# Loads of the next rows ahead of a store's wait, and transposes and affine steps split around a sum, in the first four attention blocks of a one-core block kernel

## The chip, the cores and the metric

The kernel runs on one core of a Trainium2 chip. A core has five engines that work side by side: TensorE (PE, with its weight loads PEld), VectorE (DVE), ScalarE (ACT), GpSimd (POOL) and SyncE (SP). SP only starts transfers here; POOL also starts some. Each engine runs its instructions in program order and waits at semaphores for the others. The metric is device time in microseconds (us), lower is better: the median of several executions of the whole kernel.

## The reference, cut to what matters

Two sequences of 2048 tokens with 512 features pass through an attention-like stage and a feed-forward stage (FFN), each with a normalised and modulated input and a gated residual.

```python
mod = (silu(c) @ wmod).reshape(2, 6, 1, -1)        # sa, ca, ga, sb, cb, gb
ga, gb = sign * maximum(abs, 0.25)                 # of the gates
h = layernorm(x) * (1 + ca) + sa
# attention part:
Q = relu(rope_rotate(h @ W_Q))                     # rotates the first 64 features
H = tanh(Q + hh_b)
out = group_norm(H, 32 groups of 16) * gn_weight + gn_bias
out = swapaxes(out, -2, -1).reshape(B, T, C)       # transposed, then read as rows
x = x + ga * out
# FFN part:
h = layernorm(x) * (1 + cb) + sb
w_gate, w_up, w_down = lut[gate_idx], lut[up_idx], lut[down_idx]   # 16-entry table
x = x + gb * ((silu(h @ w_gate.T) * (h @ w_up.T)) @ w_down.T)
```

## The kernel before, in words

The 2048 tokens of a sequence are cut into four blocks of 512 tokens, and the work of a block sits in tiles of 128 partitions x 512. The kernel runs the four attention blocks of the first sequence, then the FFN in groups of two blocks, with the attention blocks of the second sequence between FFN steps. Every product with a weight is made of three float16 products (high part times high part, high times low, low times high), so every operand exists as a high and a low half.

The change is in the first part, the four attention blocks of sequence 0. The first three are called regular here (q = 0, 1, 2), the fourth is the last. Beside a block's own work these blocks build the first FFN weights: for a chunk w of 512 columns, ACT or POOL turns loaded indices into float16 (`half_idx`), DVE compares them with eight values (`masks`), PE multiplies the resulting one-hot tiles by diagonal matrices (`sum_chunk`, 16 matrix products), and ACT writes the result to the weight store (`summed_out`, four instructions). Four chunks go with each block.

A block q consists of these steps, each on one engine:

- SP loads the tokens of the block into the only buffer for it, `xa` (`load_x`); it may do so when the four transposes of the rows before are done.
- DVE computes the layer norm's numbers (`stats`), ACT applies them in place (`norm`), PE transposes the tiles (`transpose_x`, four groups k = 0 to 3 of eight instructions on two groups), ACT applies scale and shift into one of two buffers `h32` and copies the float16 high half (`affine`, in halves of two k each), POOL subtracts to get the low half (`split_lo`).
- PE multiplies by W_Q in four tiles (`project`), DVE rotates and applies the relu (`rope_relu`), ACT applies the tanh, DVE removes the group means (`center`), ACT squares, DVE sums (`sum_squares`) and scales by the group's deviation (`group_scale`, with masks of a later chunk between its small steps).
- PE transposes the result (`transpose_g`); DVE adds it to the rows in `R` (`residual`). PE's transposes k = 2 and 3 reuse the banks of 0 and 1, so they wait for the first and second of residual's four instructions.
- The rows in `R` are the input x plus a bias row that depends on the gate: SP loads x (`load_rows`), and POOL starts a transfer that accumulates the bias onto it in memory (`add_bias_rows`). `residual` waits for that transfer (semaphore `rows_added`). The bias itself is written once by ACT (`make_bias`, four instructions) and sent to `bias_dram` by SP (`store_bias`).
- SP waits for the residual and stores the rows (`x2_of_block`).

The order of all this is written out by hand in the function of each engine, so an engine's order is the order of the calls. Within a block, the steps of block q stand beside `stats`, `norm`, `transpose_x`, `affine` and `split_lo` of block q + 1, since the projection of block q + 1 needs them.

Of the kernel before, what the change touches and what calls it, by code (L numbers as in the profile page):

```python
# [95 lines left out]
def build(nc, x, wq, hh_b, gn_w, gn_b, lut, idx, c_t, wmod, cos, sin, out):  # L96
# [6 lines left out]
    with ExitStack() as ctx:  # L103
# [144 lines left out]
        def _(sp):  # L248
            def load_x(src, m):

                reach(sp, xt_ready, K * m)
                sp.dma_start(xa[:], src).then_inc(x_in, 16)
# [59 lines left out]
                sp.dma_start(bias_dram[b], bias_rows[b]).then_inc(bias_out, 16)  # L312

            for q in range(NB):
                if 0 < q < NB - 1:
                    load_x(x_toks[0, q + 1], q + 1)
                if q + 1 < NB:
                    reach(sp, x2_out, 16 * q)
                    load_rows((q + 1) % 2, rows_of_block(0, q + 1))
                last = q == NB - 1  # L320
                if last:
                    store_bias(1)
                    load_early_rows()
                if q == 0:
                    load_idx(AHEAD, 0)
                    store_bias(0)
                for w in range(AHEAD * (q + 1) + (q == 0), AHEAD * (q + 2) - last):
                    load_idx(w, w % 2)
                for s in ((), (SB,), (CB, GB), ())[q]:
                    load_mod(s)  # L330
                if not last:
                    sp.wait_ge(x2_ready, K * (q + 1))
                    sp.dma_start(x2_of_block(0, q), R[q % 2].rearrange("p (q n) -> p q n", q=A)).then_inc(x2_out, 16)
                else:
                    for k in range(K):
                        sp.wait_ge(x2_ready, K * q + k + 1)
                        src, done = ((xa[:, A - 1], x2_out), (xb[:, A - 1], x2_next))[k] if k < 2 else \
                            (R[q % 2][:, k * C:(k + 1) * C], x2_rest)
                        sp.dma_start(x2_rows[0, k][:, q], src).then_inc(done, 16)
# [72 lines left out]
        @block.gpsimd  # L412
        def _(pool):
            nc.gpsimd.memset(ident[:], 0.0).then_inc(id_zero, 1)
            pool.wait_ge(id_zero, 1)
            nc.gpsimd.affine_select(out=ident[:], in_=ident[:], compare_op=ALU.not_equal, fill=1.0, base=0,
                                    pattern=[[-1, P]], channel_multiplier=1).then_inc(id_ready, 1)
            pool.wait_ge(id_ready, 1)
            nc.gpsimd.tensor_tensor(esel[:], ident[:, 0:HALF], ident[:, HALF:P], ALU.add).then_inc(esel_ready, 1)
            pool.wait_ge(esel_ready, 1)  # L420
            pool.wait_ge(lut_split, 1)
            for h in range(2):
                for v_ in range(V):
                    ins = nc.gpsimd.tensor_scalar(diag[:, v_, h * HALF:(h + 1) * HALF], esel[:],
                                                  lutQ[:, h, v_:v_ + 1], None, ALU.mult)
            ins.then_inc(diag_ready, 1)
            pool.wait_ge(wq_max, 1)
            nc.gpsimd.partition_all_reduce(c_wqall, c_wqmax, P, RMAX).then_inc(wq_all, 1)

            def half_idx(w, par):  # L430

                reach(pool, onehot_ready, w - 1)
                pool.wait_ge(idx_in[par], (w - par) * 16 + 32)
                nc.gpsimd.tensor_scalar(idx16[par], idx_sum[par], shift[:], None, ALU.add).then_inc(idx16_late, 1)

            def split_lo(m, hi, lo, halves=(0, 1)):

                for k in (2 * h + i for h in halves for i in range(2)):
                    pool.wait_ge(hi_ready, K * m + k + 1)
                    nc.gpsimd.tensor_tensor(lo[:, k], h32[:, k % 2], hi[:, k], ALU.subtract).then_inc(lo_ready, 1)  # L440

            def table_lo(w, par):

                pool.wait_ge(w_hi, w - SUMMED + 1)
                hi, lo = (W[h][:, bass.ds(w * BLK, BLK)] for h in range(2))
                nc.gpsimd.tensor_tensor(lo, pairs[par][0], hi, ALU.subtract).then_inc(w_built, 1)

            def add_bias_rows(n, b):

                r = R_A[n] % 2  # L450
                pool.wait_ge(rows_in[r], 16 * (R_A[n] // 2 + 1))
                pool.wait_ge(bias_out, 16 * (b + 1))
                nc.gpsimd.dma_start(R[r][:], bias_dram[b], accum_op=ALU.add).then_inc(rows_added[r], 16)


            for q in range(NB - 1):
                add_bias_rows(q, 0)
                split_lo(q + 1, hq[0], hq[1])
            add_bias_rows(NB - 1, 0)
            w = AHEAD * NB  # L460
            half_idx(w + 1, 1)
            half_idx(w + 2, 0)
            split_lo(LN_B[0], h2[0][:, 0], h2[1][:, 0])
            split_lo(LN_B[1], h2[0][:, 1], h2[1][:, 1])

            for u in range(S * J):
                at = u * BLK
                pool.wait_ge(hid_hi_ready, u + 1)
                nc.gpsimd.tensor_tensor(hid[1][:, at:at + BLK], hd[:, u % S], hid[0][:, at:at + BLK],
                                        ALU.subtract).then_inc(hid_ready, 1)  # L470
                w = SUMMED + (u + 1) // 2
                if u % 2 == 0:
                    table_lo(w, w % 2)
            for g in range(G):
                if g == 1:
                    split_lo(LN_A[NB], hq[0], hq[1])
                    for n in range(NB, 2 * NB):
                        add_bias_rows(n, 1)
                        if n + 1 < 2 * NB:
                            split_lo(LN_A[n + 1], hq[0], hq[1])  # L480
                if g + 1 < G:
                    for s in range(S):
                        split_lo(LN_B[(g + 1) * S + s], h2[0][:, s], h2[1][:, s])
# [3 lines left out]
        def _(act):  # L487
# [24 lines left out]
            def tanh(n, a):  # L512
                act.wait_ge(pre_tanh, A * n + a + 1)
                nc.scalar.activation(H[:, a], H[:, a], ACT.Tanh, scale=c_isq).then_inc(tanh_ready, 1)
# [82 lines left out]
            def attn_block(q, last):  # L597
                w = AHEAD * q
                tanh(q, 0)
                if q:  # L600
                    half_idx(w + 3, 1)
                tanh(q, 1); square(q, 0); tanh(q, 2)
                if q == 0:
                    half_idx(w + 3, 1)
                square(q, 1)
                if q == 0:
                    tanh(q, 3)
                    act.wait_ge(row_ready, 1)
                    make_bias(0)
                if not last:  # L610
                    norm(q + 1)
                if q:
                    tanh(q, 3)
                summed_out(w, 0)
                square(q, 2); square(q, 3)
                if not last:
                    half_idx(w + 4, 0)
                summed_out(w + 1, 1)
                if not last:
                    affine(q + 1, CA, SA, 0, hq[0], lambda: act.wait_ge(q_ready, A * q + A))  # L620
                    half_idx(w + 5, 1)
                else:
                    half_idx(w + 4, 0)
                    copy_mod(2, (SB, CB, GB))
                summed_out(w + 2, 0)
                if not last:
                    summed_out(w + 3, 1)
                    half_idx(w + 6, 0)
# [102 lines left out]
        def _(dve):  # L731
# [294 lines left out]
            def attn_block(q, half, last):  # L1026
                w = AHEAD * q
                if q == 0:
                    rope_relu(q, q, 0)
                    gate_rows(1)  # L1030
                    rope_relu(q, q, 1)
                    gates_of_attn()
                    center(q, 0)
                    rope_relu(q, q, 2)
                    masks(w + 1, 1)
                    center(q, 1)
                    rope_relu(q, q, 3)
                else:
                    masks(w + 1, 1)
                    rope_relu(q, q, 0); rope_relu(q, q, 1); center(q, 0); rope_relu(q, q, 2); center(q, 1)  # L1040
                if not last:
                    stats(q + 1)
                if q:
                    rope_relu(q, q, 3)
# [110 lines left out]
        def _(pe):  # L1155
# [135 lines left out]
            def attn_block(q, last=False, gates=False):  # L1291
# [14 lines left out]
                if last:  # L1306
                    pe.wait_ge(q_taken, A * NB)
                    mod_product((SB, CB, GB))
                    transpose_g(q, q)
                else:  # L1310
                    transpose_x(q + 1, q)
                sum_chunk(w + 2, 0)
                if last:
                    mod_vec(2, (SB, CB))
                if not last:
# [126 lines left out]
```

## Time and profile before

| | us |
|---|---|
| median of 3 runs | 1008.93 (1008.84 to 1010.18) |
| the profiled execution, its time | 1010.04 |
| the profiled execution, its span | 1008.2 |
| PE busy | 924.3 (92%) |
| DVE busy | 597.6 (59%) |
| ACT busy | 432.1 (43%) |
| POOL busy | 137.1 (14%) |

The span runs from the first to the last instruction of the profiled execution. The regular attention blocks lie between about 40 and 169 us of it; the FFN's matrix products begin at 249.67 us. An average over the span hides that: the three blocks are another kind of work than the rest, and the change is only there. A timeline row reads: start, duration, engine, line, operation, output from input, shape, number of instructions merged, and in brackets how long the engine sat idle before and what released it.

### The profile page before, as it was taken

How to read it: one execution, taken by the hardware profiler on the slowest of the kernel's cores; microseconds unless marked ns; L12 is line 12 of the kernel's file. 1: busy time of each engine (PE TensorE's matmuls, PEld its weight loads, DVE VectorE, ACT ScalarE, POOL GpSimd, SP SyncE). 2: the span in 40 equal slices, each digit the busy share in tenths (PEclk: the TensorE clock that was granted, in tenths of full speed). 3: DMA queues.
4: the chain of work that ended last, by engine and by line, in shares of the span. 5: the costliest groups of instructions: out<-in, count | busy, mean ns of one | idle time of the engine just before them, and what ended most of it. 6: DMA issues, size and time to landing. Idle time of an engine off the chain costs nothing.

```text
span 1008.2 us, 12879 instructions
## 1 busy us (share of the span) xinstructions
PE 924.3 (92%) x4364; PEld 431.8 (43%) x4364; DVE 597.6 (59%) x1379; ACT 432.1 (43%) x652; POOL 137.1 (14%) x127
## 2 busy tenths in 40 slices
PE   4948668868999999999999999999999999999998
PEld 1324334333444444444444444444444444444443
DVE  5988989994899983338988863322223332222312
ACT  2475757468877742256255233312223331222200
POOL 3011202033333321122022001100000110000000
PEclk9969788989999999999999999999999999999999
DMA  8658365720000032240533314230000212000001
GB/s 283 189 125 230 99 193 167 236 78 32 22 21 26 15 136 84 92 136 13 167 72 98 81 47 194 74 104 0 0 0 1 73 42 95 0 0 0 11 32 42
DMA packets 33738, 83.44 MB, mean 83 GB/s; under 512 B 2848, under 2 KB 2976, under 8 KB 30624
## 3 DMA queue, kind: packets, MB, share of 16 engines
q1 hardware_dynamic: 32544, 74.54, 22.4%
q0 software_dynamic: 1152, 8.39, 4.5%
q8 instruction: 21, 0.34, 0.1%
q14 instruction: 21, 0.17, 0.1%
HBM read 64.04 MB, written 18.87 MB: 82 GB/s over the span
## 4 chain that ended last, share of the span: by engine, by line
PE 68%; DVE 16%; ACT 6%; issue 5%; DMA 5%; SPq 0%; POOL 0%; DVEq 0%; ACTq 0%
PE ps L1211 33%; PE ps L1247 22%; PE ps L1200 4%; DMA xa<-x_dram 4%; PE ps L1178 3%; DVE hid L846 3%; DVE st L765 2%; PE ps L1166 2%; PE ps L1223 2%; DVE R L832 1%; ACT xa L493 1%; ACT w_all L555 1%; ACT h L503 1%; PE ps L1258 1%; DMA w_all<-wmod_dram 1%
## 5 line engine op out<-in xcount | busy, mean ns | idle before, releaser
L1211 PE MATMUL ps<-h,w_all 128*128 128x512 f16 x1920 | 416.5, 379 | 3.3 <-ACT w_all L555 2.5
L1211 PEld LDWEIGHTS ps<-h,w_all 128*128 (+1 forms) x1920 | 187.7, 98 | 229.5 <-ACT w_all L555 3.0
L1247 PE MATMUL ps<-w_all,hid 128*128 128x512 f16 x1056 | 229.7, 379 | 0.4 <-DVE w_all L1093 0.4
L1247 PEld LDWEIGHTS ps<-w_all,hid 128*128 128x128 f16 x1056 | 103.3, 98 | 123.9 <-issue 0.9
L889 DVE SCALAR_TENSOR_TENSOR hd<-ps,col,sg 128x512 f32<-128x512 f32 x80 | 59.9, 749 | 128.7 <-ACT sg L525 128.3
L525 ACT ACTIVATE sg<-ps,col 128x512 f32<-128x512 f32 x80 | 54.8, 685 | 170.6 <-PE ps L1211 170.3
L914 DVE SCALAR_TENSOR_TENSOR hd<-ps,col,gbB 128x512 f32<-128x512 f32 x32 | 24.0, 751 | 140.5 <-PE ps L1247 140.1
L493 ACT ACTIVATE xa<-xa,ln_sb 128x512 f32<-128x512 f32 x60 | 44.0, 805 | 125.9 <-DVE ln_sb L775 125.9
L1200 PE MATMUL ps<-hid,w_all 128*128 128x512 f16 x352 | 89.1, 415 | 8.1 <-DVE hid L846 8.0
L540 ACT ACTIVATE hid<-hd 128x512 f16<-128x512 f32 (+1 forms) x88 | 55.0, 628 | 85.7 <-DVE hd L889 69.7
L1178 PE MATMUL ps<-WQ,work 128*128 128x512 f16 x384 | 85.4, 379 | 6.3 <-DVE work L794 3.2
L440 POOL TENSOR_TENSOR h<-h,h 128x512 f16<-128x512 f32 x32 | 38.3, 1217 | 305.1 <-ACT h L510 305.1
L846 DVE TENSOR_SCALAR hid<-hid 128x1024 f16<-128x1024 f16 x176 | 70.8, 461 | 15.0 <-PE ps L1200 15.0
L1166 PE MATMUL ps<-ident,xa 128*128 128x128 f32 x240 | 36.3, 301 | 42.6 <-ACT h L503 26.3
L907 DVE TENSOR_TENSOR hid<-hd,hid 128x512 f32 (+1 forms) x66 | 45.3, 691 | 47.5 <-ACT hid L540 47.5
L503 ACT ACTIVATE h<-ps,vec 128x512 f32<-128x512 f32 x64 | 47.7, 775 | 40.5 <-PE ps L1166 20.5
L440 POOL TENSOR_TENSOR work<-h,work 128x512 f16<-128x512 f32 x28 | 35.2, 1276 | 200.0 <-ACT work L510 189.1
L1200 PEld LDWEIGHTS ps<-hid,w_all 128*128 128x128 f16 x352 | 36.9, 106 | 57.4 <-issue 14.7
L1178 PEld LDWEIGHTS ps<-WQ,work 128*128 128x128 f16 x384 | 37.0, 98 | 51.9 <-DVE work L794 4.7
L555 ACT ACTIVATE w_all<-ps 64x512 f16<-64x512 f32 x88 | 52.1, 592 | 12.3 <-PE ps L1200 11.3
L1166 PEld LDWEIGHTS ps<-ident,xa 128*128 128x128 f32 x240 | 30.1, 154 | 50.9 <-ACT h L503 28.2
L765 DVE BATCH_NORM_STATS2 st<-xa 128x6 f32<-128x512 f32 x60 | 37.0, 681 | 7.7 <-DMA xa<-x_dram 7.6
(116 smaller groups left out, 766.1 us busy)
## 6 DMA issues: line engine op xcount, KB each, us to landing
R<-x_dram SPq DMA_DIRECT2D x16, 1024.0 KB, 6.9
xa<-x_dram SPq DMA_DIRECT2D x14, 1024.0 KB, 5.6
hid<-idx_dram SPq DMA_DIRECT2D x44, 256.0 KB, 5.5
R<-bias_dram POOLq DMA_DIRECT2D x8, 1024.0 KB, 9.0
out_dram<-R SPq DMA_DIRECT2D x32, 256.0 KB, 2.2
x_dram<-R SPq DMA_DIRECT2D x7, 1024.0 KB, 5.1
w_all<-wmod_dram SPq DMA_DIRECT2D x6, 1024.0 KB, 13.2
h<-idx_dram SPq DMA_DIRECT2D x11, 256.0 KB, 2.6
```

What stands on the lines that cost most here:

```text
L440: nc.gpsimd.tensor_tensor(lo[:, k], h32[:, k % 2], hi[:, k], ALU.subtract).then_inc(lo_ready, 1)
L503: nc.scalar.activation(h32[:, k % 2], bank(banks[k % len(banks)]), ACT.Identity, bias=vec[:, shift, k, b:b + 1], scale=vec[:, scale, k, b: ...
L540: nc.scalar.activation(hid[0][:, bass.ds((j * S + s) * BLK, BLK)], hd[:, s], ACT.Copy) \
L555: ins = nc.scalar.activation(W[h][rows, bass.ds(w * BLK, BLK)], bank(GU[2 * par + half])[h * HALF:(h + 1) * HALF], ACT.Copy)
L765: ins = v.bn_stats(st[:, a], x_[:, a])
L846: ins = v.tensor_scalar(onehot[par][:, v_], idx16[par], float(v_), None, ALU.is_equal)
L889: v.scalar_tensor_tensor(hd[:, s], bank(GU[2 * s + 1]), c_kappa, sg[:, s], ALU.mult, ALU.mult) \
L1166: ins = nc.tensor.transpose(bank(banks[k % len(banks)])[:, a * P:(a + 1) * P], x_[:, a, k * P:(k + 1) * P], ident[:])
L1178: ins = nc.tensor.matmul(bank(QY[a % 2]), hq[hp][:, k, a * P:(a + 1) * P], WQ[wp][:, k], start=(k == 0 and i == 0), stop=(k == K - 1 and i ...
L1200: ins = nc.tensor.matmul(bank(GU[2 * par + half]), diag[:, v_], onehot[par][:, v_, half], start=v_ == 0, stop=v_ == V - 1)
L1211: ins = nc.tensor.matmul(bank(GU[2 * s + t]), W[wp][:, bass.ds(at, P)], h2[hp][:, s, k], start=(k == 0 and i == 0), stop=(k == K - 1 and i ...
L1247: ins = nc.tensor.matmul(bank(QY[par]), hid[hp][:, bass.ds(at, P)], W[wp][:, w_at:w_at + BLK], start=(j == 0 and i == 0), stop=(j == J - 1 ...
```

## The change

Five edits, all for sequence 0:

- SP: block q + 2's tokens are loaded ahead of the wait for block q's residual, not behind its store.
- POOL: the first accumulation of the bias (block 0) stands behind block 1's `split_lo`, not ahead of it. The others keep their places.
- ACT, block 0: `make_bias` stands behind `norm`, a square and the first `summed_out`, not ahead of them; the square of tile 1 stands behind `norm`.
- DVE, block 0: `stats` of block 1 stands ahead of `center` of tile 1.
- PE and ACT, blocks 0 to 2: the second half of `transpose_x` stands behind the third chunk's sum, and the second half of `affine` behind that chunk's `summed_out`.

```diff
@@ SP @@
             for q in range(NB):
-                if 0 < q < NB - 1:
-                    load_x(x_toks[0, q + 1], q + 1)
                 if q + 1 < NB:
                     reach(sp, x2_out, 16 * q)
                     load_rows((q + 1) % 2, rows_of_block(0, q + 1))
...
                 for w in range(AHEAD * (q + 1) + (q == 0), AHEAD * (q + 2) - last):
                     load_idx(w, w % 2)
+                if q + 2 < NB:
+                    load_x(x_toks[0, q + 2], q + 2)
                 for s in ((), (SB,), (CB, GB), ())[q]:
                     load_mod(s)
@@ POOL @@
-            for q in range(NB - 1):
+            for q in range(1, NB):
+                split_lo(q, hq[0], hq[1])
+                if q == 1:
+                    add_bias_rows(0, 0)
                 add_bias_rows(q, 0)
-                split_lo(q + 1, hq[0], hq[1])
-            add_bias_rows(NB - 1, 0)
@@ ACT @@
                 if q == 0:
                     half_idx(w + 3, 1)
-                square(q, 1)
-                if q == 0:
                     tanh(q, 3)
+                    norm(q + 1)
+                    square(q, 1)
+                    summed_out(w, 0)
                     act.wait_ge(row_ready, 1)
                     make_bias(0)
-                if not last:
-                    norm(q + 1)
-                if q:
+                else:
+                    square(q, 1)
+                    if not last:
+                        norm(q + 1)
                     tanh(q, 3)
-                summed_out(w, 0)
+                    summed_out(w, 0)
...
                 if not last:
-                    affine(q + 1, CA, SA, 0, hq[0], lambda: act.wait_ge(q_ready, A * q + A))
+                    affine(q + 1, CA, SA, 0, hq[0], lambda: act.wait_ge(q_ready, A * q + A), halves=(0,))
                     half_idx(w + 5, 1)
+                    summed_out(w + 2, 0)
+                    affine(q + 1, CA, SA, 0, hq[0], lambda: None, halves=(1,))
                 else:
                     half_idx(w + 4, 0)
                     copy_mod(2, (SB, CB, GB))
-                summed_out(w + 2, 0)
+                    summed_out(w + 2, 0)
@@ DVE @@
                     masks(w + 1, 1)
+                    rope_relu(q, q, 3)
+                    stats(q + 1)
                     center(q, 1)
-                    rope_relu(q, q, 3)
...
-                if not last:
+                if q and not last:
                     stats(q + 1)
@@ PE @@
-                    transpose_x(q + 1, q)
+                    transpose_x(q + 1, q, halves=(0,))
                 sum_chunk(w + 2, 0)
+                if not last:
+                    transpose_x(q + 1, q, halves=(1,))
```

POOL, from its last step before block 0 to the accumulation for block 2. `R<-bias_dram` is the accumulating transfer of `add_bias_rows`, `work<-h,work` the subtraction of `split_lo`.

```order
 L428 ISA col<-col 128x1
-L453 DMA R<-bias_dram 128x2048
 L440 ISA
 L440 TENSOR_TENSOR work<-h,work 128x512 x4
-L453 DMA R<-bias_dram 128x2048
+L453 DMA R<-bias_dram 128x2048 x2
 L440 TENSOR_TENSOR work<-h,work 128x512 x4
 L453 DMA R<-bias_dram 128x2048
```

The first accumulation, for block 0, now stands behind the four subtractions of block 1 and directly ahead of the one for block 1.

ACT in block 0, from the last tanh to the end of the block: first before, then now. L493 and L494 are `norm`, L519 and L520 `square`, L555 and L556 `summed_out`, L577 and L578 `make_bias`, L503/L510 and L504/L511 `affine`, L547 and L548 `half_idx`.

```order
L577 ACTIVATE h_0<-gaB,gnb 128x512 x4
L493 ACTIVATE xa<-xa,ln_sb 128x512 x4
L555 ACTIVATE w_all<-ps 64x512 x4
L519 ACTIVATE sq<-work 128x512 x2
L547 ACTIVATE hid<-hid,shift 128x1024
L555 ACTIVATE w_all<-ps 64x512 x4
L503 ACTIVATE h<-ps,vec 128x512 x2
L510 ACTIVATE work<-h 128x512 x2
L503 ACTIVATE h<-ps,vec 128x512 x2
L510 ACTIVATE work<-h 128x512 x2
L547 ACTIVATE hid<-hid,shift 128x1024
L555 ACTIVATE w_all<-ps 64x512 x8
```

```order
L494 ACTIVATE xa<-xa,ln_sb 128x512 x4
L520 ACTIVATE sq<-work 128x512
L556 ACTIVATE w_all<-ps 64x512 x4
L578 ACTIVATE h_0<-gaB,gnb 128x512 x4
L520 ACTIVATE sq<-work 128x512 x2
L548 ACTIVATE hid<-hid,shift 128x1024
L556 ACTIVATE w_all<-ps 64x512 x4
L504 ACTIVATE h<-ps,vec 128x512 x2
L511 ACTIVATE work<-h 128x512 x2
L548 ACTIVATE hid<-hid,shift 128x1024
L556 ACTIVATE w_all<-ps 64x512 x4
L504 ACTIVATE h<-ps,vec 128x512 x2
```

`make_bias` stands five instructions later, and between the two halves of `affine` there now are one `half_idx` and one `summed_out`; the last two copies and the fourth `summed_out` follow.

## Rows read from the trace of the kernel before

**Rows 1.** Windows: busy time of each engine, granted clock (PEclk), DMA

```profile
81.20:124.30 43.10, 31.31 (x145) 15.57 (x144) 38.72 (x107) 28.01 (x42) 6.77 (x5) 0.84 0.59 168
250.00:1008.00 758.00, 743.25 (x3584) 348.05 (x3581) 391.90 (x810) 279.41 (x424) 90.38 (x77) 1.00 0.17 56
```

**Rows 2.** Chain of waits, its piece behind block 0's residual and store: start, us, what

```profile
81.66 10.74 DMA xa<-x_dram
```

**Rows 3.** Timeline of DVE, blocks 0 to 2

```profile
45.10 2.77 DVE L846 TENSOR_SCALAR hid<-hid 128x1024 f16<-128x1024 f16 x8
...
73.68 4.70 DVE L846 TENSOR_SCALAR hid<-hid 128x1024 f16<-128x1024 f16 x8 [2.28 <-PE ps L1200]
78.31 2.90 DVE L832 SCALAR_TENSOR_TENSOR R<-ps,gnw,R 128x512 f32<-128x512 f32 x4
...
85.70 0.24 DVE L790 TENSOR_TENSOR gs<-ps,cosT 128x64 f32<-128x64 f32 x1 [0.43 <-PE ps L1178]
...
92.43 2.47 DVE L765 BATCH_NORM_STATS2 st<-xa 128x6 f32<-128x512 f32 x4 [1.21 <-DMA xa<-x_dram]
...
117.51 3.61 DVE L846 TENSOR_SCALAR hid<-hid 128x1024 f16<-128x1024 f16 x8 [1.15 <-PE ps L1200]
121.48 2.91 DVE L832 SCALAR_TENSOR_TENSOR R<-ps,gnw,R 128x512 f32<-128x512 f32 x4 [0.36 <-PE ps L1190]
...
136.80 2.47 DVE L765 BATCH_NORM_STATS2 st<-xa 128x6 f32<-128x512 f32 x4 [2.28 <-DMA xa<-x_dram]
161.88 3.62 DVE L846 TENSOR_SCALAR hid<-hid 128x1024 f16<-128x1024 f16 x8 [1.15 <-PE ps L1200]
```

**Rows 4.** Timeline of ACT, block 0, and one row of block 1

```profile
51.24 2.55 ACT L577 ACTIVATE h<-gaB,gnb 128x512 f32<-128x512 f32 x4
55.79 2.93 ACT L493 ACTIVATE xa<-xa,ln_sb 128x512 f32<-128x512 f32 x4 [2.00 <-DVE ln_sb L775]
...
61.18 1.15 ACT L519 ACTIVATE sq<-work 128x512 f32<-128x512 f32 x2
62.35 1.15 ACT L547 ACTIVATE hid<-hid,shift 128x1024 f16<-128x1024 int32 x1
63.52 2.40 ACT L555 ACTIVATE w_all<-ps 64x512 f16<-64x512 f32 x4
65.95 1.45 ACT L503 ACTIVATE h<-ps,vec 128x512 f32<-128x512 f32 x2
67.30 1.15 ACT L510 ACTIVATE work<-h 128x512 f16<-128x512 f32 x2
...
110.58 1.15 ACT L510 ACTIVATE work<-h 128x512 f16<-128x512 f32 x2
```

**Rows 5.** Timeline of POOL, blocks 0 and 1

```profile
71.27 2.27 POOL L440 TENSOR_TENSOR work<-h,work 128x512 f16<-128x512 f32 x2 [10.87 <-issue]
75.01 2.76 POOL L440 TENSOR_TENSOR work<-h,work 128x512 f16<-128x512 f32 x2 [1.47 <-ACT work L510]
77.72 1.05 POOL L453 DMA_DIRECT2D R<-bias_dram  x1
...
115.35 3.13 POOL L440 TENSOR_TENSOR work<-h,work 128x512 f16<-128x512 f32 x2 [1.47 <-ACT work L510]
```

**Rows 6.** DMA issued at 59.19, 77.72 and 118.44: KB, us to landing

```profile
R<-bias_dram POOLq DMA_DIRECT2D x1, 1024.0 KB, 9.3
...
R<-bias_dram POOLq DMA_DIRECT2D x1, 1024.0 KB, 9.2
...
R<-bias_dram POOLq DMA_DIRECT2D x1, 1024.0 KB, 12.7
```

**Rows 7.** Windows after an idle stretch of PE: PE busy first, PEclk third from last

```profile
66.78:68.75 1.97, 1.97 (x9) 1.85 (x10) 1.94 (x8) 1.66 (x3) 0.00 (x0) 0.50 0.97 216
68.75:73.60 4.85, 4.85 (x18) 1.89 (x16) 2.59 (x3) 0.78 (x1) 2.27 (x2) 0.71 0.08 18
73.60:77.10 3.50, 3.50 (x19) 1.68 (x17) 3.42 (x7) 3.45 (x6) 2.09 (x2) 1.00 0.00 0
```

## The prediction

> **What bounds the kernel now.** I read the windows first. From 250 us on PE is busy 743.25 of 758.00 us at full clock, while in block 1's stretch it is busy 31.31 of 43.10 us and DVE 38.72 [rows 1]. So in the regular blocks DVE sets the pace, and the change can only return what DVE sits idle there, plus what a new wait costs. What the blocks win or lose is handed on whole to the FFN, which starts on what they leave.
>
> Then the waits and the timeline of DVE, for its idle time. It waits twice for the tokens of the next block, 1.21 us in block 1 and 2.28 in block 2 [rows 3], 3.5 in all. Behind each block's last group step it waits 1.15 us for a sum of PE, and in block 1 another 0.36 for the transposes ahead of `residual` [rows 3]. The chain of waits shows where the tokens' lateness comes from: block 0's residual ends at 81.21 (78.31 + 2.90) [rows 3], the store is issued, and the load behind it, at 81.66, takes 10.74 us [rows 2].
>
> Last the timelines of ACT and POOL in block 0 and the landing times, for the step that `residual` waits for and that none of the above waits shows: the accumulation of the bias. Before, the first one was issued at 59.19 and took 9.3 us [rows 6], so it was there at 68.5, ten microseconds ahead of the residual at 78.31 [rows 3].
>
> **Part 1: the load of tokens ahead of the wait.** It leaves SP when the index loads of the block are out and the transposes done, some 8 us earlier in block 0 and more in block 1. The cover that it needs is there: `stats` of block 2 could not start before 91.2 (92.43 less 1.21) [rows 3]. Both waits go: -1.21 and -2.28, together -3.5 us. The instructions are the same; what is behind it on SP, the store, waits for the residual anyway.
>
> **Part 2: the halves in blocks 1 and 2.** The third sum now fills PE's wait for the first affine half and is over before DVE's group step, so the 1.15 us go, and the 0.36 with them: at most 1.5 us a block. But ACT now does a `half_idx` (1.15) and a `summed_out` (2.40) between the halves [rows 4]. In block 1's own clock: the first copies end at 111.73 [rows 4], + 1.15 + 2.40 + 1.45 for the affine pair (adding up to 116.7), and POOL begins about 0.6 later, at 117.3, where it began at 115.35 [rows 5]. That puts all of its 3.13 us beside DVE's masks, which can start at 116.36 (117.51 less 1.15) [rows 3]. What such overlap costs is in block 0: eight masks take 2.77 alone and 4.70 where POOL's 2.76 lie inside them [rows 3, 5], so in these 2.76 us DVE got through 0.83 us of masks, 30%. Here: 0.94 us free, then 3.13 us at 30% (0.94), then the remaining 0.89 us: they end near 121.3, where the residual before started at 121.48. So the halves give 0.2 us a block, not 1.5. With no overlap cost it would be 1.5 (plus 0.8 for the overlap of before, 3.61 less 2.77); with POOL running later still, -0.5. I take 0.2 each, -0.4 for two blocks, bounds -4.6 to +1.
>
> **Part 3: block 0.** Here I follow ACT. `stats` moves ahead of one `center` (two DVE steps, about 1.3 us), so `norm` starts at about 54.5 instead of 55.79 and ends at 57.4. Then a square 0.6, `summed_out` 2.40 (60.5), `make_bias` 2.55 (63.05), two squares (64.3), `half_idx` 1.15 (65.45), `summed_out` 2.40 (67.85), first affine half 1.45 and copies 1.1 (70.4), `half_idx` 1.15 (71.55), `summed_out` 2.40 (73.95), second half's affine pair 1.45, and the copies from 75.3 [durations from rows 4]. POOL starts its last two subtractions at about 76.0 and needs 2.6 to 3.1 us: 78.9.
>
> POOL's 10.87 us of issue ahead of its first subtraction [rows 5] begin behind the transfer at 59.19; now nothing stands between and they fall in the idle time before. That was worth about 3 us to ACT's second half (copies from 67.30, subtraction at 71.27 and not 68.0), and is given back by the steps put between. The residual could start at about 78.5, as before.
>
> But it can't, since the accumulation for its rows is now issued only at 78.9. The two accumulations without other traffic took 9.3 and 9.2 us, the one beside a modulation load, a store and a token load 12.7 [rows 6]. In the new place the token load is out since about 73 and nearly landed; only the second accumulation follows 1.1 us behind, on the same queue. I take 9.3: landing at 88.2, against a residual at 78.31. DVE waits there, PE's third transpose stands behind the residual, and block 1's projection behind that: nothing hides it. +9.9 us, bounds +8 (POOL done at 77.5, landing 9.0) and +13.3 (12.7).
>
> A page speaks against this size. The Trainium skill ("DMA: Bandwidth & Descriptors", section on the anatomy of one DMA on the SWDGE path) gives a transfer issued from GpSimd about 2.0 us plus the bytes at 436 GB/s; an estimate by that page for 1 MB is 4.4 us. The trace does not agree for the accumulating transfer, which took 9.2 us and more each time. By the page the total below would be about 5 us lower.
>
> **Part 4: PE's clock behind the new wait.** PE has its first two transpose groups done by about 77 and then nothing until 88.9. After an idle stretch of only 6 us before, its granted clock was 0.50 and then 0.71 of full: 1.97 + 4.85 us went into work that at clock 1.00 takes about 1.0 (half of 1.97) + 3.50 (16 products of a sum, as in the next window) [rows 7]. So 2.3 us are lost, on the third and fourth transposes and the first tiles of block 1's projection. DVE has masks (2.77) to do meanwhile, but it waited 0.43 us for tile 1 before, with PE at full clock [rows 3], so all of it comes through: +2.3, bounds 0.9 and 3.
>
> **Sum** against the profiled execution: -3.5 - 0.4 + 9.9 + 2.3 = +8.3 us. Its time is 1010.04, so 1018.3; the median of the runs is 1.1 lower, and on its scale the time is 1008.93 + 8.3 = 1017.2. I forecast 1017.
>
> **Rivals.**
> - *The accumulation is hidden after all.* If it were on chip by the time of the residual, only parts 1 and 2 and their better case would remain: -3.5 and -0.4 to -3: 1002.5 to 1005, say 1004.5. For it: POOL's long issue time goes, and ACT's second half could run earlier than I have it. Against it: it would have to be issued by 69, and four subtractions whose inputs ACT makes after 73.95 stand ahead of it. It decides from the point at which issue plus 9.3 is earlier than 78.5. 8%.
> - *The loss is there, but smaller.* The accumulation moves 1 MB and nothing competes with it; if it takes half of the shortest row, 4.6 us, the sum is 4.6 less: +3.7, 1012.6. Against it: that row, 9.2, was issued into idle queues too [rows 6]. 8%. The Trainium skill's rule above ("DMA: Bandwidth & Descriptors") leads to this case.
> - *The gains are larger.* POOL's subtractions do not hit the masks: -1.5 -0.8 twice instead of -0.4: 1017.2 - 4.2 = 1013. For it: the masks' start at 116.36 and POOL's at 117.3 are each known to half a microsecond only. 12%.
> - *The landing is slow.* The second accumulation's packets go between the first's, and it takes the 12.7 of the loaded case: +3.4, 1020.5. 12%.
> - *The token load in front of the store brings nothing*, since a later step was going to hold DVE anyway: +3.5, also near 1020.5. In the trace nothing ends within these waits but the load, so only 3%.
>
> **Chances.** The forecast, 1015 to 1019, has 57%, the rivals 43%. The 80% range leaves out the hidden case and the tails of the others: 1011.5 to 1020.7. About 0.2%, 2 us, is what a measurement can tell. Faster than 1006.9: only the first rival, 8%. Within 2 us: the corner of the second and third together, 7%. Slower: 85%.
>
> **What would show it.** In the changed profile DVE's first instruction of `residual` in block 0 should have about 10 us of idle time before it, released by the DMA from `bias_dram`, and start near 88. POOL's accumulations should stand together near 79 and 80. PE's granted clock should fall to 0.5 near 89, with block 1's second tile late by 12 us. The waits for `xa` should be gone. In blocks 1 and 2 the eight masks ahead of the residual should have no idle time before them but last 4 to 5 us. I am wrong if the first accumulation is issued before 70 or lands within 6 us, or if residual 0 starts by 80; and if block 1 takes under 40 us from residual to residual, part 2 was undervalued.

## The result: 1.1% slower

| | before | changed |
|---|---|---|
| median of 4 runs each, us | 1009.17 | 1019.74 (1019.34 to 1022.11) |
| profiled execution, us | 1010.04 | 1019.6 |
| its span, us | 1008.2 | 1017.8 |

The ratio of changed to before is 1.0108, with a 95% interval of 1.009 to 1.0125. Measured again later it was 1.0107 (1.0092 to 1.0121). The forecast was 1017 us, or 8.3 us more than before, with 1011.5 to 1020.7 as its range; measured were 10.6 us more between the medians and 9.6 between the profiled executions.

The step on which most of it rested is in DVE's timeline of the changed kernel, which answers to [rows 3]. L837 is now `residual`, L851 `masks`, L795 the first step of `rope_relu`, L770 `stats`.

```profile
74.07 4.68 DVE L851 TENSOR_SCALAR hid<-hid 128x1024 f16<-128x1024 f16 x8
86.41 1.41 DVE L837 SCALAR_TENSOR_TENSOR R<-ps,gnw,R 128x512 f32<-128x512 f32 x2 [7.66 <-DMA R<-bias_dram]
...
95.33 0.23 DVE L795 TENSOR_TENSOR gs<-ps,cosT 128x64 f32<-128x64 f32 x1 [1.11 <-PE ps L1184]
...
100.75 2.46 DVE L770 BATCH_NORM_STATS2 st<-xa 128x6 f32<-128x512 f32 x4
...
124.61 4.69 DVE L851 TENSOR_SCALAR hid<-hid 128x1024 f16<-128x1024 f16 x8
129.22 1.39 DVE L837 SCALAR_TENSOR_TENSOR R<-ps,gnw,R 128x512 f32<-128x512 f32 x2
131.16 1.60 DVE L837 SCALAR_TENSOR_TENSOR R<-ps,gnw,R 128x512 f32<-128x512 f32 x2 [0.55 <-PE ps L1196]
...
138.90 0.23 DVE L795 TENSOR_TENSOR gs<-ps,cosT 128x64 f32<-128x64 f32 x1 [1.11 <-PE ps L1184]
```

DVE sat idle 7.66 us ahead of block 0's residual, until the bias accumulation had landed. `stats` at 100.75 has no wait in brackets: the wait for the tokens is gone. Both sets of masks ahead of a residual run without a wait, but for 4.7 us instead of 2.77. And the rope steps of the second tile (the two with L795) each have 1.11 us of waiting for PE.

POOL's timeline (answers to [rows 5]) and one piece of the chain of waits show the accumulation: two are issued from 78.09, and the first takes 8.30 us.

```profile
69.33 2.34 POOL L440 TENSOR_TENSOR work<-h,work 128x512 f16<-128x512 f32 x2 [45.98 <-ACT work L511]
75.54 2.60 POOL L440 TENSOR_TENSOR work<-h,work 128x512 f16<-128x512 f32 x2 [3.86 <-ACT work L511]
78.09 2.09 POOL L453 DMA_DIRECT2D R<-bias_dram  x2
```

```profile
78.09 8.30 DMA R<-bias_dram
```

PE's timeline around the residuals of blocks 0 and 1. L1196 is `transpose_g`, eight instructions for two of the four groups, and L1184 the projection of the next block.

```profile
87.22 1.97 PE L1196 MATMUL ps<-ident,work 128*128 128x128 f32 x8 [11.06 <-DVE R L837]
88.98 11.42 PE L1184 MATMUL ps<-WQ,work 128*128 128x512 f16 x48
...
130.01 1.97 PE L1196 MATMUL ps<-ident,work 128*128 128x128 f32 x8 [4.01 <-DVE R L837]
131.77 12.20 PE L1184 MATMUL ps<-WQ,work 128*128 128x512 f16 x48
```

In block 1 of the kernel before, where L1190 is `transpose_g` and L1178 the projection, the same instructions read:

```profile
120.76 1.04 PE L1190 MATMUL ps<-ident,work 128*128 128x128 f32 x8
122.28 1.32 PE L1190 MATMUL ps<-ident,work 128*128 128x128 f32 x8 [0.49 <-DVE R L832]
123.56 10.53 PE L1178 MATMUL ps<-WQ,work 128*128 128x512 f16 x48
```

There the second eight transposes take 1.32 us and the projection 10.53, with a granted clock of 1.00 and a gap of only 0.49 us ahead of them. In the changed kernel PE was idle 11.06 us ahead of the first and 4.01 us ahead of the second, and both were followed by slow work. The windows of the changed kernel behind the second (columns as in [rows 7]) put the granted clock at 0.50 and 0.60.

```profile
130.00:131.80 1.80, 1.79 (x9) 1.73 (x10) 1.25 (x2) 0.48 (x1) 0.00 (x0) 0.50 1.08 284
131.80:136.00 4.20, 4.20 (x13) 1.57 (x12) 3.54 (x10) 0.00 (x0) 0.00 (x0) 0.60 0.92 192
```

How far DVE is behind the kernel before, at the same instructions of both profiled executions, gives the sum by terms. The last column tells what accounts for the change from the row above it.

| instruction of DVE | before | changed | behind | what lies between |
|---|---|---|---|---|
| residual 0 | 78.31 | 86.41 | 8.10 | late accumulation, +8.1 |
| rope of tile 1, block 1 | 85.70 | 95.33 | 9.63 | slow clock, +1.5 |
| stats for block 2 | 92.43 | 100.75 | 8.32 | wait for tokens gone, -1.3 |
| residual 1 | 121.48 | 129.22 | 7.74 | halves, -0.6 |
| rope of tile 1, block 2 | 129.01 | 138.90 | 9.89 | slow clock, +2.2 |
| stats for block 3 | 136.80 | 144.32 | 7.52 | wait for tokens gone, -2.4 |
| residual 2 | 165.85 | 172.78 | 6.93 | halves, -0.6 |
| rope of tile 1, block 3 | 173.26 | 182.86 | 9.60 | slow clock, +2.7 |
| end of the span | 1008.2 | 1017.8 | 9.6 | nothing |

### The profile page after: what moved, and what is told of

It reads as the page before. It is cut to its first block, busy times and chain, and to the rows that moved or that the text cites. A ratio compares the mean times of both kernels' runs of the same rounds, so it can differ in the third digit from the quotient of the medians.

```text
span 1017.8 us, 12880 instructions
## 1 busy us (share of the span) xinstructions
PE 930.6 (91%) x4364; PEld 432.2 (42%) x4364; DVE 605.1 (59%) x1379; ACT 430.3 (42%) x652; POOL 135.3 (13%) x127
## 4 chain that ended last, share of the span: by engine, by line
PE 66%; DVE 19%; ACT 6%; issue 5%; DMA 4%; POOL 1%; SPq 1%; DVEq 0%; ACTq 0%; POOLq 0%
PE ps L1217 33%; PE ps L1253 22%; PE ps L1184 4%; DVE hid L851 4%; DVE st L770 2%; PE ps L1229 2%; DMA xa<-x_dram 1%; ACT xa L494 1%; DMA w_all<-wmod_dram 1%; PE ps L1172 1%; PE ps L1206 1%; DVE R L837 1%; ACT w_all L556 1%; DVE gs L758 1%; ACT h L504 1%
## 5 line engine op out<-in xcount | busy, mean ns | idle before, releaser
L494 ACT ACTIVATE xa<-xa,ln_sb 128x512 f32<-128x512 f32 x60 | 44.0, 803 | 123.3 <-DVE ln_sb L780 123.3
L1184 PE MATMUL ps<-WQ,work 128*128 128x512 f16 x384 | 90.0, 393 | 4.5 <-DVE work L799 3.2
L851 DVE TENSOR_SCALAR hid<-hid 128x1024 f16<-128x1024 f16 x176 | 76.6, 493 | 6.6 <-PE ps L1206 6.6
L504 ACT ACTIVATE h<-ps,vec 128x512 f32<-128x512 f32 x64 | 47.4, 774 | 33.2 <-PE ps L1172 20.5
L1184 PEld LDWEIGHTS ps<-WQ,work 128*128 128x128 f16 x384 | 38.4, 101 | 53.6 <-issue 8.2
L556 ACT ACTIVATE w_all<-ps 64x512 f16<-64x512 f32 x88 | 52.0, 590 | 9.5 <-PE ps L1206 8.5
L1172 PE MATMUL ps<-ident,xa 128*128 128x128 f32 x240 | 32.8, 281 | 16.7 <-ACT xa L494 10.0
L515 ACT ACTIVATE work<-work,col 128x512 f32<-128x512 f32 x32 | 23.0, 719 | 55.1 <-DVE work L801 55.1
L1196 PE MATMUL ps<-ident,work 128*128 128x128 f32 x128 | 19.9, 304 | 25.0 <-DVE R L837 19.1
```

Source lines behind the costliest of these rows:

```text
L494: ins = nc.scalar.activation(x_[:, a], x_[:, a], ACT.Identity, bias=ls[:, 3, a:a + 1], scale=ls[:, 2, a:a + 1])
L504: nc.scalar.activation(h32[:, k % 2], bank(banks[k % len(banks)]), ACT.Identity, bias=vec[:, shift, k, b:b + 1], scale=vec[:, scale, k, b: ...
L556: ins = nc.scalar.activation(W[h][rows, bass.ds(w * BLK, BLK)], bank(GU[2 * par + half])[h * HALF:(h + 1) * HALF], ACT.Copy)
L851: ins = v.tensor_scalar(onehot[par][:, v_], idx16[par], float(v_), None, ALU.is_equal)
L1184: ins = nc.tensor.matmul(bank(QY[a % 2]), hq[hp][:, k, a * P:(a + 1) * P], WQ[wp][:, k], start=(k == 0 and i == 0), stop=(k == K - 1 and i ...
```

## The experiments

Each is given with its ratio to the kernel before in runs on the same chip, and the 95% interval. The kernel before had medians of 1010.38, 1010.26 and 1010.23 us in the three batches, with single runs from 1008.0 to 1013.6.

### Block 0 undone

```diff
 # the kernel before, plus: load_x of q + 2 ahead of the wait for residual q,
 # transpose_x and affine in halves around the third sum
 # as before: add_bias_rows(0) ahead of split_lo(1), make_bias ahead of norm
```

> The kernel before with the early token loads and the halves on PE and ACT, but with block 0 on POOL, ACT and DVE as before (bias accumulation ahead of the subtractions, make_bias early). My theory: the loss of block 0 comes from the late accumulation, so it goes; of the rest, the two token waits give 3.5 us and the overlap gain 1.2, and PE's slow clock behind the idle gap that the halves open costs 2 us or more in each block: 1009 to 1012. Rival 1 (the loss lies in the halves in all blocks): 1015 or more. Rival 2 (halves as I forecast them, no clock cost behind blocks 1 and 2): 1005.

Measured: 1011.71 us, 1.0015 (1.0003 to 1.0026). Block 0's part costs the difference to 1.0107, some 9.3 us, against 8.1 + 1.5 in the table. The result lies where the theory had it and in neither rival's place: the loss is not in the halves alone, and yet these two parts, for which the prediction had a gain of 3.9 us, gave none. PE's timeline of this kernel has the slow clock behind block 1's residual too:

```profile
122.25 1.97 PE L1192 MATMUL ps<-ident,work 128*128 128x128 f32 x8 [4.03 <-DVE R L834]
124.02 12.68 PE L1180 MATMUL ps<-WQ,work 128*128 128x512 f16 x48
```

### The loads alone

```diff
-                if 0 < q < NB - 1:
-                    load_x(x_toks[0, q + 1], q + 1)
...
+                if q + 2 < NB:
+                    load_x(x_toks[0, q + 2], q + 2)
```

> The kernel before with the token loads ahead of the residual's wait, nothing else. Theory: both waits of DVE for xa go and nothing takes their place: 3.5 us less, 1005.6. Rival (something else holds DVE there anyway, or the load's traffic delays the index loads or the accumulation): within 1 us of before.

Measured: 1007.16 us, 0.9974 (0.9962 to 0.9986), 1.4 to 3.8 us less than before. DVE has no wait for `xa` left in these blocks. This part of the change does what was forecast for it.

### The halves alone

```diff
-                    transpose_x(q + 1, q)
+                    transpose_x(q + 1, q, halves=(0,))
                 sum_chunk(w + 2, 0)
+                if not last:
+                    transpose_x(q + 1, q, halves=(1,))
 # and on ACT the affine in halves around half_idx and summed_out
```

> The kernel before with only the halves on PE and ACT in blocks 0 to 2. Theory: about 0.6 us a block won at the residual, lost again with 2 us or more a block to PE's projection at half clock, and DVE waiting about 1 us for each of its first two tiles: 1012 to 1014. Rival (no clock cost): 1008.5. The wait for xa remains, and part of the loss may hide in it.

Measured: 1011.89 us, 1.0017 (1.0007 to 1.0027), 0.7 to 2.7 us more. The direction is the theory's, the size about half. DVE waits for single tiles by 0.7 to 1.3 us behind each residual, and as expected part of that is taken out of the wait for the tokens, which no longer shows.

### POOL's order alone

```diff
+            for q in range(1, NB):
+                split_lo(q, hq[0], hq[1])
+                if q == 1:
+                    add_bias_rows(0, 0)
                 add_bias_rows(q, 0)
```

> The kernel before with only POOL's order changed: the first bias accumulation behind block 1's four subtractions. make_bias stays early. Theory: POOL's subtractions start about 3 us earlier, the accumulation is issued near 76 to 78 and lands 8.3 us later, so residual 0 starts at 84 to 86 instead of 78.3, and block 1's projection runs its start at half clock: 1009 + 7 to 9 = 1016 to 1018. Rival (the late make_bias is what holds the accumulation): 1009 or less.

Measured: 1014.31 us, 1.0039 (1.0023 to 1.0054). The accumulation is issued at 75.45 and takes 8.2 us; DVE's timeline shows the wait:

```profile
83.68 1.41 DVE L833 SCALAR_TENSOR_TENSOR R<-ps,gnw,R 128x512 f32<-128x512 f32 x2 [5.78 <-DMA R<-bias_dram]
```

The residual is 5.4 us late and starts at 83.68, about where the theory had it (84 to 86), and slow tiles behind it add another 1.9 us, but the time is only 3.9 more, not 7 to 9. By DVE's instructions in the two profiled executions, 1.8 us are taken back at the two waits for tokens, which shrink from 1.21 to none and from 2.28 to 1.77, and 1.2 us ahead of the next two residuals, where PE's two sums took 7.94 and 8.47 instead of 9.09 us; the edit gives no reason for the latter, and it may be chance. So a delay put in early is not handed on whole as long as a later wait can absorb it. In the changed kernel the loads had already removed the waits for tokens.

### PE kept busy in its gaps

```diff
+                    transpose_g(q, q + 1, halves=(0,))
+                    if not gates:                      # blocks 1 and 2
+                        pe.wait_ge(q_taken, A * q + A)
+                        for i in range(16):
+                            nc.tensor.matmul(bank(QY[1]), WQ[0][:, i % K, 0:P], WQ[0][:, i % K],
+                                             start=True, stop=True)
+                    transpose_g(q, q + 1, halves=(1,))
```

> The changed kernel, with 16 matrix products more on PE in blocks 1 and 2 (WQ by WQ into a free bank, results unused) between the second and the third of the transposes ahead of the residual. They add 3.5 us of work to a gap of 4.0 us. Theory (PE's clock is half behind that gap, and costs DVE about 2.4 us in each of the two blocks): projection rows of 10.5 us instead of 12.2 and 12.6, DVE's waits of 1.1 us at the second tile gone, and 4 to 5 us less than the changed kernel. Rival (the slow projection has another cause, such as its inputs): no faster, or slower by the added work.

Measured: 1016.64 us, 1.0066 (1.0054 to 1.0078), against 1.0107 for the changed kernel: 4.1 us less (by these two intervals, 2 to 6) with 32 matrix products more, as the theory had it. PE's timeline in block 1 of this kernel:

```profile
126.43 3.62 PE L1329 MATMUL ps<-WQ 128*128 128x512 f16 x16
130.72 1.22 PE L1196 MATMUL ps<-ident,work 128*128 128x128 f32 x8 [0.68 <-DVE R L837]
131.91 10.53 PE L1184 MATMUL ps<-WQ,work 128*128 128x512 f16 x48
```

The added products fill 3.62 of the 4 us, and the projection takes 10.53 us instead of 12.20; in block 2 it takes 10.52 instead of 12.60. DVE's waits at the second tile shrink from 1.11 us to 0.50 and 0.37. That is the experiment that shows the cause of the term that the prediction missed: it changes nothing but what PE does in the gap.

### POOL's configuration ahead of its wait

```diff
             nc.gpsimd.partition_all_reduce(c_wqall, c_wqmax, P, RMAX).then_inc(wq_all, 1)
+            pool.wait_ge(diag_ready, 1)
+            nc.gpsimd.tensor_tensor(esel[:], ident[:, 0:HALF], ident[:, HALF:P], ALU.add)
```

> The kernel before with one small elementwise instruction on POOL behind the all-reduce, its result unused. Theory: the 10.9 us of issue time ahead of POOL's first subtraction is the change of POOL's configuration, which follows the first accumulation in program order; it now falls into idle time, so the first subtraction starts near 68.0 instead of 71.3, and the residual of block 0, held by PE's sums more than by POOL, comes 0.5 to 1 us earlier: 0.7 us less than before. Rival (the issue time belongs to what follows a transfer that POOL starts): nothing moves.

Measured: 1007.23 us, 0.9979 (0.997 to 0.9989), 1.1 to 3.0 us less. POOL's first subtraction, 71.27 with 10.87 us of issue before [rows 5], is now released by its input:

```profile
68.52 2.59 POOL L442 TENSOR_TENSOR work<-h,work 128x512 f16<-128x512 f32 x2 [7.60 <-ACT work L512]
```

So most of the issue time belongs to the change of configuration, which waited behind the accumulation in program order. Not all of it is accounted for: in its new place the small instruction has 7.03 us of issue ahead of it, and where the other 3.8 us of the 10.87 come from is not shown; the rival may hold for them. The time fell by more than the 0.7 us of the theory, but block 0's residual moved only from 78.31 to 78.11. The gain came later. By DVE's instructions in the two profiled executions, 1.5 us come at the two waits for tokens (none and 1.85 us instead of 1.21 and 2.28) and 1.2 us ahead of residuals 1 and 2, where PE's two sums took 7.86 and 8.37 instead of 9.09 us. Why the small instruction should do either was not tested.

The Trainium skill ("GPSIMD Engine Reference", section "Instruction dispatch") puts the load of freshly loaded code at about 6 us. Of the issue times on POOL in these traces, the first, ahead of the all-reduce, agrees with 5.85 us; the 7.03 and 10.87 us are longer.

### The second half ahead of summed_out

```diff
-                    half_idx(w + 5, 1)
-                    summed_out(w + 2, 0)
-                    affine(q + 1, CA, SA, 0, hq[0], lambda: None, halves=(1,))
+                    half_idx(w + 5, 1)
+                    affine(q + 1, CA, SA, 0, hq[0], lambda: None, halves=(1,))
...
+                summed_out(w + 2, 0)
```

> As e1_undo_block0 (early loads, halves, block 0 as before), but on ACT the summed_out of the third chunk stands behind the second affine half, not ahead of it. Theory: POOL's last two subtractions come 2.4 us earlier and no longer beside DVE's masks, which then last near 3 us instead of 4.7; the residual comes 1.5 us earlier in each block and PE's gap ahead of it shrinks from 4 to 2.5 us: 3 to 5 us less than e1_undo_block0, so 2 to 3 less than before. Rival (POOL does not slow the masks): as e1_undo_block0.

Measured: 1011.38 us, 1.0012 (1.0002 to 1.0022): the time is the rival's (as the first kernel of this section), not the theory's. But the rival's reason, that POOL does not slow the masks, is not what the trace shows. POOL's last two subtractions now start 0.93 us ahead of the masks, where they started 0.83 us behind their start, but they take 3.32 us instead of 2.56, and 2.4 us of that still lie beside the masks:

```profile
115.11 3.32 POOL L440 TENSOR_TENSOR work<-h,work 128x512 f16<-128x512 f32 x2 [1.47 <-ACT work L510]
```

```profile
116.04 4.69 DVE L847 TENSOR_SCALAR hid<-hid 128x1024 f16<-128x1024 f16 x8
```

The masks take 4.69 us again, and PE's gap stayed at 4.1 us. So the move was too small to take POOL off the masks.

### The residual ahead of the masks

```diff
                     group_scale(q, 0, 1)
-                    masks(w + 4, 0)
...
                 residual(q, half, (xa[:, A - 1], xb[:, A - 1]) if last else ())
+                if not last:
+                    masks(w + 4, 0)
 # otherwise as the kernel above
```

> As e7_act_late, and DVE's residual stands ahead of the masks of the next block's first chunk in the regular blocks. Theory: PE's gap between the transposes closes, its clock stays full, the projection starts some 3 us earlier under DVE's two sets of masks, and DVE's waits for the first tiles go: 6 to 8 us less than before. Rival (DVE is the bound and only changes its order, the waits for the transposes take the place of the others): 3 us less than before, as e2_load_only.

Measured: 1005.84 us, 0.9958 (0.9944 to 0.9972), 2.8 to 5.6 us less than before. PE's gap between the transposes is 0.5 us, and the first half of the projection runs at full clock:

```profile
116.93 1.32 PE L1192 MATMUL ps<-ident,work 128*128 128x128 f32 x8 [0.49 <-DVE R L833]
118.20 5.35 PE L1180 MATMUL ps<-WQ,work 128*128 128x512 f16 x24
125.71 7.04 PE L1180 MATMUL ps<-WQ,work 128*128 128x512 f16 x24 [2.16 <-DVE work L795]
```

The third tile then waits for DVE, which does masks, and in blocks 1 and 2 the rest runs slow once more (7.04 us for 24 products instead of 5.35), behind waits of only 2.16 and 2.28 us. DVE waits 1.44 and 1.65 us for it. The granted clock in block 1 was still 1.00 in the gap and fell behind it, to 0.50 between 128 and 130 us. That is part of what keeps the gain at 4.4 us rather than the 6 to 8 of the theory; DVE's 3.90 us of waiting ahead of block 0's residual and 0.9 ahead of the other two are others, and no run takes them apart. Nor is the gain over the loads alone (0.9974) clear of the intervals.

### Both together, and the loads with the configuration

```diff
 # e9: the kernel above, plus the small instruction on POOL
 # e10: the kernel before, plus the early loads and the small instruction on POOL
```

> As e8_residual_first, with the small instruction on POOL of e6_config. Theory: e8 has 3.9 us of DVE idle ahead of block 0's residual, held by ACT's second affine half, which waits for POOL; the earlier configuration gives about 2 to 3 us of it back: 6 to 8 us less than before in all, 1003. Rival (that wait is not on the path): as e8_residual_first, 4.4 less than before.

> The kernel before with the early loads (e2_load_only, 3.2 less) and the small POOL instruction (e6_config, 3.0 less), without halves. Theory: the two act in different blocks and add up: 5 to 6 us less than before. Rival (part of each gain is the same slack, or chance in when PE's clock returns): 3 to 4 less.

Measured: 1005.47 us, 0.9946 (0.9932 to 0.9961), and 1006.21 us, 0.996 (0.9946 to 0.9974). They lie 3.9 to 6.9 and 2.6 to 5.5 us below before; with the kernel above they are the fastest three of the study, and nothing can be told apart between them. So neither theory is borne out in its size: the first is 0.4 us below the kernel above where 2 to 3 were expected, and the second, 4.0 us below before, is where the rival had it and not at 5 to 6. In the first, block 0's residual starts at 74.19 with 0.83 us of waiting, where the kernel above had 3.90 us of waiting before 75.47. Of the 3.1 us of waiting that went, 1.7 were taken by two small steps of DVE, which now lay beside POOL's earlier subtractions and took 1.14 and 1.13 us instead of 0.29 each. The second kernel moves one load, adds one instruction with its wait, and has no halves.

### The changed kernel again, and with the bias made early

```diff
                     tanh(q, 3)
+                    act.wait_ge(row_ready, 1)
+                    make_bias(0)
                     norm(q + 1)
                     square(q, 1)
                     summed_out(w, 0)
-                    act.wait_ge(row_ready, 1)
-                    make_bias(0)
```

> The changed kernel once more, beside these runs of before, as the reference for e5_warm and e12_bias_made_early: 9 to 11 us above before, with PE's projection behind the three residuals at 11 to 12.7 us, different in each execution.

> The changed kernel with make_bias on ACT where it was before in block 0. POOL's order stays: the accumulation behind the subtractions. Theory: ACT's second affine half comes 2.5 us earlier or a little less, so does the accumulation and with it the residual of block 0 (84 instead of 86.4): about 2 us less than the changed kernel. If instead the lateness of the bias in memory were what delays the landing, all of block 0's loss would go: 8 us less.

Measured: 1020.74 us, 1.0107 (1.0092 to 1.0121), and 1019.35 us, 1.0092 (1.0078 to 1.0106). The first is as expected, with projections of 11.17, 12.07 and 12.54 us. The difference between the two, 1.4 us where about 2 were expected, is within their intervals; the trace is what tells. The residual of block 0 starts 1.5 us earlier, since the accumulation is issued at 76.70 instead of 78.28. DVE still waits 6.91 us for it. So it is the place on POOL that makes the accumulation late, and not the time at which the bias is in memory.

## Why the prediction was right, and where it was not

- **The late accumulation** (part 3) was forecast at 9.9 us and measured 8.1. The mechanism is shown by the wait in DVE's timeline, and by the runs without it and with it alone. POOL was done 0.8 us earlier than worked out (at 78.1, not 78.9): 0.5 of it by ACT's copies, at 74.84 and not 75.3, the rest by POOL's shorter subtractions. The landing took 8.3 us and not 9.3. The prediction wrote that this transfer took 9.2 us and more each time, but its rows show three of eight: the last four in the same trace took 8.8, 8.0, 7.9 and 7.9 us, so that the bound of 9.0 on the landing was too high. The page's estimate of 4.4 us was of another size: behind block 1's subtractions the accumulating transfer took 8.2 to 8.3 us in four kernels; in the changed kernel the token load was in by 79.8 (issued at 72.5, 7.3 us), and from then on only the second accumulation was on its way beside it.
- **The clock behind that wait** (part 4), forecast +2.3, measured +1.5, within its bounds.
- **The loads** (part 1), forecast -3.5: -3.7 in the table, and 0.9974 (2.6 us) by themselves.
- **The halves** (part 2), forecast -0.2 a block: the residuals came 0.6 us earlier each. The reason given for their poverty, that POOL's subtractions fall onto the masks, holds: 4.69 us of masks, worked out at 4.9 (116.36 to 121.3).
- **The step that failed** is in part 2 as well, where "the 1.15 us go, and the 0.36 with them" was the last word on PE. I asked what its clock does behind the wait of block 0 and did not ask it behind blocks 1 and 2. With the halves PE is done with its sums earlier: counted from DVE's `stats`, its first pair of transposes ahead of the residual starts 24.1 us later in blocks 1 and 2, and 28.3 us in the kernel before. But DVE's masks stand ahead of the residual, so PE gets a gap of 4.0 us in each block between the second and the third transpose, where it had 0.49 before. Behind the gap the clock is at 0.50, and DVE waits for tiles: +2.2 and +2.7 us. In the kernel before, the late sums were what kept PE busy up to the residual. The run with added products shows this term by itself, at 4.1 us. It is also what turned the halves, forecast to give 0.4 us, into a loss: by themselves they cost 0.7 to 2.7 us.
- The four terms of the forecast give +8.3, the measured ones 8.1 + 1.5 - 3.7 - 1.2 = 4.7, and the missed term 4.9 brings that to 9.6. The total was nearer than its parts, and that was luck: 4.9 us were left out, and against them stood 1.8 + 0.8 us of overestimated loss and 1.0 us of underestimated gain.
- Of the rivals, the hidden accumulation and the small landing time are ruled out by DVE's 7.66 us of waiting and the landing time of 8.30. The larger gains are ruled out by the masks' 4.69 us. The slow landing did not happen: the second accumulation on the same queue did not slow the first, which took 8.30 us, within the 7.9 to 9.3 us of six of the eight in the kernel before. That the early load brings nothing is ruled out by the run with the loads alone.

What stays open is what share of the slow projection is chance. It took between 11.13 and 12.68 us behind gaps of 4.0 to 4.1 us, and the single runs of the kernel before differ by up to 5 us on one chip. PE's two sums ahead of the residual vary too: in block 1 of the kernels without halves they took 7.86 to 9.13 us, each time behind 8.3 us of idle time. The table's terms are from one execution each.

## What to carry to other kernels

When an instruction is moved behind others on the queue that starts a transfer, count the transfer's landing time from its new place and look who waits for it; here that was 8 of 10 us, with nothing removed in exchange. When a step is finished earlier, ask what its engine does until its next input: on PE, a gap of 4 us cost more than the earlier finish gave. With the consumer moved forward as well the loss was gone, but no gain over the loads alone was clear of the intervals, and the residual moved forward without the halves was not tried. And a wait that is removed also stops absorbing what is delayed upstream.

## What the runs showed of the hardware that was not expected

- A gap of 4.0 us was followed by the granted clock of 0.50, which is the lower of the two levels, and the 48 products behind it took 11.13 to 12.68 us instead of 10.52. In the kernel before, gaps of 0.49 to 1.13 us left them at 10.5. In the kernels with the residual ahead of the masks, 24 products took 5.35 and 5.36 us behind gaps of 1.82 and 2.00 us, and 7.04 behind gaps of 2.16 and 2.28. Nor is the last gap all that counts: a gap of 1.57 us left the 48 products at 10.52 (the loads alone, block 0), while one of 1.56 us, with 2.99 us of idle time and only eight transposes ahead of it, was followed by 12.29 us (the second half ahead of `summed_out`, block 0).
- The same eight masks on DVE took 2.77 us alone, 4.69 in kernels in which POOL's two subtractions lay inside them, and as much in the one in which 2.4 of POOL's 3.3 us did. The Trainium skill ("GPSIMD Engine Reference", Specifications) lists POOL's SBUF interface as shared with VectorE and in contention with some of its modes; the trace agrees, with 1.9 us more for 2.4 to 2.8 us of POOL's work beside them.
- 32 matrix products whose results nobody uses made the changed kernel 4.1 us faster.
